# Edge counts of a graph layer: windows of 8 to 40 destinations, and keys of four edge columns made in one comparison

## The reference, cut to what matters

```
_o = jnp.argsort(dst, stable=True)
src = src[_o]
dst = dst[_o]
...
deg = jax.ops.segment_sum(jnp.ones_like(dst, dtype=x.dtype), dst, num_segments=n)
inv_deg = (1.0 / jnp.clip(deg, 1.0))[:, None]
...
neigh = jax.ops.segment_sum(h[src], dst, num_segments=n) * inv_deg
h = h @ Ws_self[l] + neigh @ Ws_neigh[l] + bs[l]
```

## Time and profile before

| | us |
|---|---|
| median of 3 runs (lowest, highest) | 1332.99 (1331.43, 1338.83) |
| profiled execution, span from first to last instruction | 1331.9 |
| PE busy in it | 1255.2 (94%) |
| DVE busy in it | 557.6 (42%) |
| edge counts, from the first key (L1455) to the column sums (L450) | 15.4 to 165.3 |

### The profile page before, as it was taken

How to read it: one execution, slowest core, us unless ns; L and a number is a source line. 1 busy time by engine, 2 the same in 40 slices (tenths; PEclk the granted TensorE clock), 3 DMA queues, 4 the chain that set the end, 5 groups by cost and what they waited for, 6 DMA issues and landing times.

```text
span 1331.9 us, 19378 instructions
## 1 busy us (share of the span) xinstructions
PE 1255.2 (94%) x6567; PEld 828.1 (62%) x6568; DVE 557.6 (42%) x1512; ACT 462.4 (35%) x991; POOL 198.8 (15%) x201
## 2 busy tenths in 40 slices
PE   4899999999999989989999999999989999989797
PEld 2554467466546645548877887877655587664465
DVE  8999833111124335110000000001187345677894
ACT  5799643222112220001111111111113343338893
POOL 2000000000000004711111111111173000013480
PEclk8999999999999989989999999999998999999899
DMA  9200000000020020175134611662563000200011
GB/s 206 95 1 1 1 2 1 0 1 1 0 95 21 30 108 1 20 259 207 47 118 164 233 50 46 229 231 83 205 188 117 1 33 1 72 0 0 1 30 49
DMA packets 42949, 98.25 MB, mean 74 GB/s; under 512 B 4113, under 2 KB 6603, under 8 KB 41845
## 3 DMA queue, kind: packets, MB, share of 16 engines
q1 hardware_dynamic: 28613, 68.70, 15.5%
q0 software_dynamic: 6144, 16.45, 4.5%
q10 hardware_dynamic: 8112, 12.08, 2.5%
HBM read 81.02 MB, written 16.17 MB: 73 GB/s over the span
## 4 chain that ended last, share of the span: by engine, by line
PE 73%; DVE 13%; POOL 4%; issue 4%; ACT 2%; DMA 2%; ACTq 1%; DVEq 1%; POOLq 0%
PE psum L450 34%; PE psum L1864 14%; PE psum L1908 7%; PE psum L1840 4%; PE psum L2070 4%; POOL slot_tokens L711 3%; PE psum L478 1%; PE psum L1936 1%; PE psum L1887 1%; DVE sb_hT_conv L1455 1%; ACT sb_htok L834 1%; DVE sb_stats L458 1%; DVE sb_x_res L1269 1%; PE psum L1981 1%; POOL sb_blk L655 1%
## 5 line engine op out<-in xcount | busy, mean ns | idle before, releaser
L450 PEld LDWEIGHTS psum<-sb_blk,sb_w_reg 128*128 128x128 f32 x1792 | 204.0, 192 | 12.7 <-issue 12.7
L450 PE MATMUL psum<-sb_blk,sb_w_reg 128*128 128x128 f32 x1792 | 205.2, 275 | 1.6 <-issue 1.6
L1864 PE MATMUL psum<-sb_z_reg_r,sb_hT_conv_r 125*125 125x512 f32 x400 | 169.0, 423 | 0.6 <-DVE sb_z_last L1109 0.4
L450 PE MATMUL psum<-sb_w_reg,sb_hT_conv 128*125 128x512 f32 (+1 forms) x376 | 167.2, 594 | 0.0
L1239 DVE TENSOR_TENSOR sb_blk<-sb_blk,psum 128x256 f32<-128x256 f32 x56 | 23.6, 421 | 276.9 <-ACT sb_blk L805 276.9
L1864 PE MATMUL psum<-sb_htok_r,sb_hT_conv_r 125*125 125x512 f32 x300 | 118.8, 396 | 0.0
L450 PEld LDWEIGHTS psum<-sb_w_reg,sb_hT_conv 128*125 128x125 f32 (+1 forms) x376 | 68.3, 187 | 76.6 <-issue 75.9
L450 PE MATMUL psum<-sb_hT_conv,sb_w_reg 128*128 128x416 f32 (+3 forms) x336 | 101.8, 459 | 0.8 <-ACT sb_hT_conv L484 0.8
L1908 PE MATMUL psum<-sb_w_reg,sb_blk 128*128 128x512 f32 x224 | 100.8, 592 | 0.0
L784 ACT CAST sb_hT_conv_r<-sb_a_reg 125x625 fp32r<-125x625 f32 x80 | 56.2, 716 | 115.5 <-PE psum L1864 115.5
L1864 PEld LDWEIGHTS psum<-sb_z_reg_r,sb_hT_conv_r 125*125 125x125 f32 x400 | 74.7, 187 | 23.0 <-issue 5.4
(11 more groups left out here) (396 smaller groups left out, 1753.0 us busy)
## 6 DMA issues: line engine op xcount, KB each, us to landing
sb_hT_conv<-w_expert SPq DMA_DIRECT2D x7, 2048.0 KB, 9.9
sb_w_reg<-w_expert SPq DMA_DIRECT2D x6, 2048.0 KB, 18.2
sb_hT_conv<-w_expert SPq DMA_DIRECT2D x7, 1024.0 KB, 12.4
...
```

Source lines behind the costliest of these rows:

```text
L450: ins = e.matmul(out, l, r, start=(n == 0), stop=(n == len(pairs) - 1))
L1864: ins = e.matmul(psum[0:TP, b, :], counts_at(l, 2 * i + n // NT)[:, s % HALF_T, :], z[s], start=(n == 0), stop=(n == len(pairs) - 1))
```

## The change

The windows get eight widths, one for each ten runs: 8, 12, 18, 22, 28, 32, 36 and 40 destinations. The matmul, the addition into `adj` and the keys of a run take 10 x width columns in place of 400; key and window start are worked out with a run's own width (`win_row`, `last_base`, `past_win`).

For the first 60 runs (widths up to 32) one `tensor_tensor` comparison makes all four keys: `key_pairs` holds each number 0, 1, 2, ... twice, `key16` the keys in fp16, and the two columns of a pair lie interleaved in `hot_key`, so that PE reads them with a step of two. For these runs and the next ones with widths below 36, ACT makes two of the four `hot_lo` columns and DVE two.

The first products are spread as eight on seven runs from run 11 on, so that all 76 stand in the loop; layer norm starts one run later (`FIRST_LN` 5). `vec_z` of tiles 8 and 9 moves from behind the sums into the loop.

```diff
-PASSES = -(-N_TOK // WIN)
+CLASS = 10
+CLASS_WIN = (8, 12, 18, 22, 28, 32, 36, WIN)
+PASSES = 1 + -(-(N_TOK - min(CLASS_WIN)) // WIN)
+WIDE_LO = 36
+PAIRED = 60
+PAIR_KEYS = NT * CLASS_WIN[PAIRED // CLASS - 1]
...
+def run_win(t):
+    return CLASS_WIN[t // CLASS]
+def lo_by_act(t):
+    return 3 if run_win(t) >= WIDE_LO else 2
...
-        FIRST_LN, FIRST_Z = 4, 10
+        FIRST_LN, FIRST_Z, Z_GAP = 5, 11, 7
...
+            e.iota(key_pairs, [[1, PAIR_KEYS], [0, 2]], base=0, channel_multiplier=0,
+                   allow_small_or_imprecise_dtypes=True).then_inc(edge_pool, 1)
...
+            for n, w in enumerate(CLASS_WIN):
+                e.memset(win_row[:, n * CLASS:(n + 1) * CLASS], float(w)).then_inc(edge_pool, 1)
...
-                    c = RUN * t + 3
-                    e.tensor_scalar(hot_lo[n][:, 3, :], neg_iota, neg_lo[:, c:c + 1], None, ALU.is_equal)
-                    for j in range(RUN):
+                    for j in range(lo_by_act(t), RUN):
                         c = RUN * t + j
-                        e.tensor_scalar(hot_key[n][:, j, :], key_iota, key[:, c:c + 1], None,
-                                        ALU.is_equal).then_inc(hot_ready, 1)
+                        e.tensor_scalar(hot_lo[n][:, j, :], neg_iota, neg_lo[:, c:c + 1], None, ALU.is_equal)
+                    if t < PAIRED:
+                        of_all = [TP, RUN // 2, NT * w, 2]
+                        own = key16[:, RUN * t:RUN * (t + 1)].rearrange("p (a b) -> p a b", b=2)
+                        e.tensor_tensor(paired_keys(t), key_pairs[:, 0:NT * w, :].unsqueeze(1).to_broadcast(of_all),
+                                        own.unsqueeze(2).to_broadcast(of_all), ALU.is_equal).then_inc(hot_ready, RUN)
+                    else:
+                        for j in range(RUN):
+                            c = RUN * t + j
+                            e.tensor_scalar(hot_keys(t, j), key_iota[:, 0:NT * w], key[:, c:c + 1], None,
+                                            ALU.is_equal).then_inc(hot_ready, 1)
...
-                for i in every(t, FIRST_Z + 7, 8):
+                for i in every(t, FIRST_Z + 6, Z_GAP):
                     vec_z(e, 0, i, z_bank(0, i), z_lo_rows)
...
-            for i in range(NT - 2, NT):
-                vec_z(e, 0, i, z_bank(0, i), z_lo_rows)
...
+        def products_to(t):
+            return min(max(0, (t - FIRST_Z) * 8 // Z_GAP), 8 * NT - KD)
...
-                pe_first_product(e, t - FIRST_Z)
-            for n in range(STATIC_RUNS - FIRST_Z, 8 * NT - KD):
-                pe_first_product(e, n)
+                for product in range(products_to(t), products_to(t + 1)):
+                    pe_first_product(e, product)
+            for n in range(products_to(STATIC_RUNS), 8 * NT - KD):
+                pe_first_product(e, n)
```

More of the change, by code:

```diff
@@ L38, with squares_to @@
 STATIC_RUNS = RUNS - 1
-STEPS = 104
+CLASS = 10
[4 more added lines that the diff above has]
+PAIR_KEYS = NT * CLASS_WIN[PAIRED // CLASS - 1]
+STEPS = 92
+def run_win(t):
+    return CLASS_WIN[t // CLASS]
+def lo_by_act(t):
+    return 3 if run_win(t) >= WIDE_LO else 2
+def squares_to(t):
+    return sum(lo_by_act(r) for r in range(t))
+ALL_SQUARES = squares_to(STATIC_RUNS)
 N_GNN = 3
@@ L179, in build @@
                    for n in range(2)]
-        first_dst, base = (w_conv_flat[0:TP, 1600 + n * RUNS:1600 + (n + 1) * RUNS] for n in range(2))
+        first_dst, base, past_win, last_base = (
+            w_conv_flat[0:TP, 1600 + n * RUNS:1600 + (n + 1) * RUNS] for n in range(4))
         reach_spread = htok_flat[0:RUNS, 1536:1536 + 2 * RUNS]
@@ L491, in every, with paired_keys, hot_keys @@
             return [i] if rest == 0 and 0 <= i < NT else []
+        def paired_keys(t):
+            return hot_key[t % 2].rearrange("p j n -> p (j n)")[:, 0:RUN * NT * run_win(t)].rearrange(
+                "p (a w b) -> p a w b", a=RUN // 2, b=2)
+        def hot_keys(t, j):
+            if t < PAIRED:
+                return paired_keys(t)[:, j // 2, :, j % 2]
+            return hot_key[t % 2][:, j, 0:NT * run_win(t)]
         def z_bank(l, i):
@@ L894, in scalar @@
                         e.wait_ge(lo_ready, t - 1)
-                    for j in range(3):
+                    for j in range(lo_by_act(t)):
                         c = RUN * t + j
@@ L900, in scalar @@
                     r = t - 1
-                    e.wait_ge(lo_squared, 3 * (r + 1))
+                    k = lo_by_act(r)
+                    e.wait_ge(lo_squared, squares_to(r + 1))
                     if r >= 2:
                         e.wait_ge(adj_mm, r - 1)
-                    e.activation(hot_lo[r % 2][:, 0:3, :], sq_lo[r % 2], ACT.Relu, bias=1.0,
+                    e.activation(hot_lo[r % 2][:, 0:k, :], sq_lo[r % 2][:, 0:k, :], ACT.Relu, bias=1.0,
                                  scale=-1.0).then_inc(lo_ready, 1)
@@ L910, in scalar @@
                     act_turned(e, i, 6 + i % 2)
-                for i in every(t, FIRST_Z + 6, 8):
+                for i in every(t, FIRST_Z + 5, Z_GAP):
                     act_z_hi(e, 0, i, z_bank(0, i))
-                for i in every(t, FIRST_Z + 10, 8):
+                for i in every(t, FIRST_Z + 9, Z_GAP):
                     if i < NT - 1:
@@ L1428, in vector @@
                                 None, ALU.mult).then_inc(edge_vec, 1)
+            e.wait_ge(edge_pool, WIN_ROW)
+            e.tensor_scalar(last_base, win_row, -1.0, float(N_TOK), ALU.mult, ALU.add).then_inc(v_own, v.up())
+            e.tensor_tensor(by_run(key), by_run(tile_i), win_row.unsqueeze(2).to_broadcast([TP, RUNS, RUN]),
+                            ALU.mult).then_inc(v_own, v.up())
+            e.wait_ge(v_own, v.n)
+            e.tensor_tensor(key, key, dst_f, ALU.add).then_inc(v_own, v.up())
+            e.wait_ge(v_own, v.n)
             e.wait_ge(runs_spread, 1)
@@ L1432, in vector @@
             e.tensor_tensor(run_span, psum[0:TP, 1, RUNS:2 * RUNS], first_dst, ALU.subtract).then_inc(v_own, v.up())
+            e.wait_ge(v_own, v.n)
+            e.tensor_tensor(run_span, run_span, win_row, ALU.subtract).then_inc(v_own, v.up())
             e.wait_ge(v_own, v.n)
@@ L1486, in vector @@
                     e.drain()
-                    e.tensor_tensor(win_at[:, 0:1], first_dst[:, bass.ds(r, 1)], win_at[:, 2:3], ALU.add)
+                    e.tensor_tensor(win_at[:, 0:1], past_win[:, bass.ds(r, 1)], win_at[:, 2:3], ALU.add)
                     e.drain()
```

47 lines of the change are left out of this document (29 added, 18 removed).

## The result

The changed kernel took 1325.35 us (median of 4, 1323.23 to 1327.06) against 1333.37 for the kernel before (median of 4, 1331.43 to 1338.83): a ratio of 0.9937, interval 0.9918 to 0.9957. The prediction said 1324.0 (1318.5 to 1335.5), faster by more than 0.5%. That it is faster is clear of noise; that it is so by more than 0.5% is likely and not certain, since the interval reaches 0.9957. The profiled execution has a span of 1321.5 us, against 1331.9.

What follows compares the result with a forecast made beforehand. DVE was taken as the bound, PE 0.04 us behind. The loop's 11.1 us gain plus 0.5 behind it, less 2.7 for the cold clock, gave 8.9, rounded 9.0, so 1324.0 us (1318.5 to 1335.5).

Steps and rivals of the forecast that it cites:

- DVE bounds, PE is 0.04 behind, and PE bounds from run 27 on: In the loop: DVE needs 1.58 us a run, PE 1.54; after the change PE becomes dense and DVE shows idle time.
- The price of 0.52 ns: DVE's paired comparison: two 16-bit sources cost 0.52 ns an element, half the 1.04 of f32.
- A: Rival: the paired comparison runs at one element a cycle, 1.04 ns, making the kernel slower, 1339; chance 0.12.
- B: Rival: re-reading each key pair raises the comparison's price to 0.9 ns, so time stays even, 1333; chance 0.05.
- The gate by DMA: Before PE's first product: it waits for `w_gnn` by DMA and begins at about 38.5 us, whatever the engines do.
- The start, 0.7 us: Ahead of the loop: added small operations, split keys and POOL's work lengthen the way by about 0.7 us, hidden by DMA.
- The loop: From 38.5 us: larger of DVE and PE per stretch, 102.7, plus 1.5 cold clock and 3.0 hand-offs; run 78 ends at 145.7.
- ACT stays below the others: In the loop: ACT needs about 1.0 us a run with two squares, coming close only in the last 19 runs.
- rival C: Rival: hand-offs between three near-equal engines lose 0.1 us in each of 67 runs, 6.7 not 3; 1328 to 1330; chance 0.10.
- Cold clock, first time: At PE's first products: after idling PE starts at half clock, 1.2 GHz, which costs 1.5 us.
- Behind the loop: Run 78 to flag: about 0.5 us gained by DVE adding at once, 2.7 lost to PE's cold clock.
- Net at the flag: At the flag's multiplication: 11.1 us from the loop plus 0.5 minus 2.7 gives 8.9 earlier, rounded 9.0.

Runs made afterwards that it cites:

- p3: Changed kernel with a run's keys left in f32, so paired comparisons have one f32 source; ratio to the kernel before 1.0048.
- p1: Changed kernel with narrow windows but every run's four keys made one by one, not in pairs; ratio to the kernel before 0.9954.
- p0: The changed kernel measured once more, as it stands, as yardstick; 1328.52 us, ratio to the kernel before 0.9926.
- run 30: No follow-up kernel: a turn of the kernel's own loop, counted from 0; the yardstick p0 begins it at 67.85 us.
- q1: Changed kernel with the key-pair table copied by ACT from the plain iota instead of POOL's paired iota; ratio to the kernel before 0.9926.
- r3: Changed kernel with ACT's key-pair table, and first-layer weights loaded alone ahead of biases and remaining weights; ratio to the kernel before 0.9901.
- run 78: No follow-up kernel: the last turn but one of the loop's 80; through at 145.7 us in the changed kernel, 156.8 before.
- s1: r3 with one first-layer product a run, started earlier, ACT's casts and copies and DVE's low parts a step later, earlier layer norm; 1315.61 us, ratio to before 0.983.
- run 12: No follow-up kernel: an early turn of the kernel's own loop, counted from 0, with a window 12 wide.
- run 79: No follow-up kernel: the last of the loop's 80 turns, ahead of the column sums; its four matmuls took 1.78 us in the changed kernel.
- p5: Changed kernel with first-layer products one a run, eight behind the loop, last two low parts behind the last run; ratio to the kernel before 0.9919.

## Why the prediction was right, and where it wasn't

The time came out 1.35 us from the forecast, and the sign and the main mechanism are shown. That it is so near is in part luck, as said at the end. Step by step:

- **DVE bounds, PE is 0.04 behind, and PE bounds from run 27 on.** Right. p3 makes DVE the bound again, and its loop is 15.5 us longer; p1, with dearer keys on DVE, is as fast as p0 from run 30 on.
- **The price of 0.52 ns.** Right, 0.518. Rivals A and B, the slower side, fell with it; p3 shows that A was priced right to 1 us.
- **The gate by DMA.** The mechanism was right: q1 changes the start by 3.5 us and the first product by nothing. The time was 1.5 us off (37.07, forecast 38.5). It landed at 36.88 to 37.59 in the eight traces of kernels that have the changed kernel's loads and narrow windows; why at 38.56 before, is open. Not seen was that the gate is the kernel's own doing, biases and the second weights beside the first: r3 opens it, for 4.8 us.
- **The start, 0.7 us.** Wrong in size: 4.6. The small operations did cost 0.7. The iota in pairs was priced by the small ones of its kind, and took 3.61; it pushed POOL's memset beside DVE's cast, 3.8 more. So the "wait of 5 us or more" was 1.58, and the cover nearly used up.
- **The loop.** Run 78 ended at 145.7, to the tenth as forecast, though from 1.4 us earlier: 108.7 us where the sum gives 107.2. The terms, by the starts of PE's runs: 30 to 39 took 14.95 (forecast 13.5), 40 to 49 14.9 (14.6), 50 to 59 16.8 (15.5), 60 to 69 16.3 (15.9), 70 to 78 14.7 (15.0); ten runs hold one or two of the double products, which is up to 0.5 us up or down of each. The term that was mis-sized is the larger of DVE and PE for each stretch: a second product, a low part, and a cast that waits follow each other through buffers of two, and don't lie beside each other. The 3.0 us for hand-offs took up most of it. The prediction's own sign for this (ACT ending waits in the last 19 runs) appeared once, for 0.6 us, of 2.1 in the whole loop. The step that failed is "ACT stays below the others", which counted ACT's work and not the place of its casts; s1 shows what the places cost, all of them together.
- **Hand-offs, rival C** (0.1 a run): 1.5 us beyond the forecast's 3.0, so between the two.
- **Cold clock, first time.** 1.5 forecast. The first product lost 1.0 us, the second about 0.5, and the four matmuls of run 12 0.2: about 1.7, up to the third product at 41.39, which took 0.91.
- **Behind the loop.** The sums lost 1.53 (forecast 2.5), since the clock rose after 3.3 us of them and not after 5; in other traces with the gap they took 7.2 to 8.2 us. Run 79's matmuls took 0.9 more, but the clock's part in that is the forecast's 0.2: at 1.00 they took 1.43 in s1, and the addition behind them waits 0.79 us for PE against 0.58 there. Together 1.7 for 2.7. Against that, run 78's end to the sums' start is 153.06 - 145.7 = 7.3, before 165.31 - 156.8 = 8.5: 1.2 gained net of the 0.2, where the forecast had 0.5 gross. It charged 0.6 for the moved low part, and that cost nothing: from the last addition to the general loop's first operation DVE takes 1.82 us with it and 1.79 without (p5), because DVE's idle time ahead of that operation shrinks from 1.22 to 0.65.
- **Net at the flag** 10.7, forecast 8.9. Nearly all of it shows in the two profiled spans (10.4), 8.0 in the medians.

So the gate (1.4 us early) and the loop (1.5 too long) cancelled at run 78, which is luck, and the tail lost 0.4 (11.1 at run 78, 10.7 at the flag) where the forecast had 2.2. That the medians then came out within 1.35 us is luck once more: 1.8 us gained beyond the forecast at the flag don't show in them, against a scatter of several us behind it. The late start was hidden, as the prediction said any such delay would be.
